# Relative attention on one core: distance terms turned into PSUM ahead of the products, two banks an image, constants loaded ahead of the norm

## The reference, cut to what matters

```python
x = layernorm(h)
q, k, v = x @ Wq + bq, x @ Wk + bk, x @ Wv + bv          # split in 8 heads
scores[i, j] = (q[i] . k[j] + q[i] . rel_k[clip(j - i)]) * scale
w = softmax(scores, axis=j)
y[i] = sum_j w[i, j] * (v[j] + rel_v[clip(j - i)])
h = h + y @ Wo + bo
```

## Time and profile before

| | us |
|---|---|
| Median of 3 runs | 2627.47 (2611.75 to 2633.1) |
| The profiled execution | 2611.67 |
| Its span, first to last instruction | 2609.9 |
| Granted clock of TensorE, mean over the span | 0.922 |
| Norm ahead of the stage, from the first table load | 1529.4 to 1557.0 |
| Relative attention: constants | 1557.9 to 1569.9 |
| Projections and far scores | 1569.9 to 1624.9 |
| Loop over the images | 1625.1 to 1791.6 |
| Values and outputs | from 1791.7 |

### The profile page before, as it was taken

How to read it: one execution, slowest core, us unless ns; L and a number is a source line. 1 busy time by engine, 2 the same in 40 slices (tenths; PEclk the granted TensorE clock), 3 DMA queues, 4 the chain that set the end, 5 groups by cost and what they waited for, 6 DMA issues and landing times. The chain is left out here.

```text
span 2609.9 us, 55965 instructions
## 1 busy us (share of the span) xinstructions
PE 2198.0 (84%) x22566; PEld 1555.1 (60%) x22566; DVE 1868.2 (72%) x2584; ACT 1619.1 (62%) x2458; POOL 570.5 (22%) x263
## 2 busy tenths in 40 slices
PE   5348999999999999999954958778569999999998
PEld 2135444454444444454323746664459999999998
DVE  0543888888888888888655445673668788888886
ACT  0025888888888888888751314332157777777776
POOL 0023444444444444444210001331000000000000
PEclk9658999999999999999865979999769999999999
DMA  4017777777777777777611000000122222212220
GB/s 172 0 45 199 210 204 213 220 208 218 216 205 206 211 215 217 209 219 216 166 41 41 1 8 3 1 1 21 66 72 77 74 69 69 69 69 74 71 69 34
DMA packets 110228, 306.64 MB, mean 117 GB/s; under 512 B 20334, under 2 KB 56936, under 8 KB 109209
## 3 DMA queue, kind: packets, MB, share of 16 engines
q1 hardware_dynamic: 109977, 303.11, 39.7%
HBM read 170.09 MB, written 80.65 MB: 96 GB/s over the span
## 5 line engine op out<-in xcount | busy, mean ns | idle before, releaser
L579 ACT ACTIVATE la_hid<-ps,la_b 128x904 f32<-128x904 f32 (+1 forms) x480 | 450.8, 988 | 72.6 <-PE ps L434 71.7
L1515 PE MATMUL ps<-ls_xm,ls_w_in_parts 128*128 128x226 f16 x3072 | 467.7, 261 | 13.2 <-DVE ls_xm L1596 9.0
L1523 PE MATMUL ps<-ls_state_parts,ls_w_rec_parts 128*128 128x226 f16 x2976 | 448.0, 259 | 0.0
L1542 ACT ACTIVATE ls_gates<-ps,ls_bias 128x226 f32<-128x226 f32 x768 | 301.6, 446 | 127.0 <-PE ps L1523 126.9
L434 PE MATMUL ps<-la_pairs,la_w 32*64 32x452 f32 x3584 | 311.0, 573 | 45.3 <-ACT la_hid L579 42.4
L1515 PEld LDWEIGHTS ps<-ls_xm,ls_w_in_parts 128*128 128x128 f16 x3072 | 294.5, 97 | 23.1 <-issue 9.3
L1523 PEld LDWEIGHTS ps<-ls_state_parts,ls_w_rec_parts 128*128 128x128 f16 x2976 | 285.2, 96 | 6.3
L447 PE MATMUL ps<-la_hid,la_w 128*32 128x452 f32 x1856 | 248.3, 560 | 1.0 <-ACT la_opened L585 1.0
L408 POOL TENSOR_TENSOR la_P<-la_S,la_top 113x904 f32<-113x904 f32 x64 | 153.3, 2395 | 263.9 <-DVE la_top L682 263.9
L434 PEld LDWEIGHTS ps<-la_pairs,la_w 32*64 32x64 f32 x3584 | 74.3, 131 | 186.4 <-issue 113.0
L396 POOL TENSOR_TENSOR la_P<-la_P,la_inv 113x904 f32<-113x904 f32 x64 | 132.1, 2085 | 189.7 <-DVE la_inv L661 189.7
(11 more groups left out here) (294 smaller groups left out, 4247.8 us busy)
## 6 DMA issues: line engine op xcount, KB each, us to landing
la_pairs<-la_maps SPq DMA_DIRECT2D x224, 452.0 KB, 6.1
la_gate<-la_opened SPq DMA_DIRECT2D x448, 113.0 KB, 3.4
ls_w_all<-ls_weights SPq DMA_DIRECT2D x32, 904.0 KB, 4.1
la_maps<-la_ST SPq DMA_DIRECT2D x32, 791.0 KB
la_maps<-la_S SPq DMA_DIRECT2D x32, 791.0 KB
ls_m_all<-ls_masks SPq DMA_DIRECT2D x32, 456.0 KB, 3.6
la_maps<-la_Cr SPq DMA_DIRECT2D x32, 395.5 KB
la_maps<-la_Cl SPq DMA_DIRECT2D x32, 395.5 KB
```

Source lines behind the costliest of these rows:

```text
L579: act.activation(hid[:, u % 4, 0:n], ps[:, bank:bank + n, 0:HALF], ACT.Gelu_apprx_tanh, bias=b1[:])\
L1515: mm = pe.matmul(out_j, w_in_parts[:, w, e, j, :], xm[:, t % 2, e, :, x, 0:N], start=((w, x) == PASSES[0]), stop=(t == 0 and (w, x) == PAS ...
L1523: mm = pe.matmul(out_j, w_rec_parts[:, w, e, j, :], state_parts[:, x, e], start=False, stop=((w, x) == PASSES[-1]))
L1542: return act.activation(dst, ps[:, n % 3 * 2 + j // 2, j % 2 * 256:j % 2 * 256 + C], ACT.Tanh if j == 3 else ACT.Sigmoid, bias=bias[:, e, ...
```

## The change

- The constants' tiles are made first, and a block of their own, with SyncE alone, loads them; then `norm_and_turn` runs, called from within `relative_attention`; then the rest. The other engines wait for `consts_in` where they did.
- GpSimd waits for `bias_set`, VectorE's signal after `q_bias`, before it adds `b_out` to `h`.
- The products of an image take two banks, four heads each, and there are three such sets (banks 0 to 5). Image b uses set b mod 3.
- `distances(b)` is new: eight transposes (`is_transpose`) of the distance terms into the image's two banks. It waits until image b - 3 is subtracted. `scores(b, part)` adds the products of q and k to them, in two halves of four heads; each half uses two of the four strips of rows, one strip a bank. The second waits for the first (`half_made`).
- `turn(b)` has one pair of banks, 6 and 7, in place of two, so it waits until image b - 1 is copied. The heads lie in another order in `z`, which `turn` undoes.
- TensorE's order: `distances(b)`, `scores(b, 0)`, `turn(b - 2)`, `scores(b, 1)`. The orders of VectorE and ScalarE stay.

```diff
     with Phase(nc, "ra") as ph:
...
+        consts_in = ph.sem("consts_in")
+        with ph.block() as block:
+            @block.sync
+            def _(sp):
+                for tile, name in loads:
+                    sp.dma_start(tile[:], dram[name]).then_inc(consts_in, 16)
+                for tile, name in rows:
+                    sp.dma_start(tile[:], dram[name].partition_broadcast(N)).then_inc(consts_in, 16)
+
+        norm_and_turn(nc, "ra_norm", h, hT, ps, ident, eps)
+
...
-                for tile, name in loads:
-                    sp.dma_start(tile[:], dram[name]).then_inc(s["consts_in"], 16)
-                for tile, name in rows:
-                    sp.dma_start(tile[:], dram[name].partition_broadcast(N)).then_inc(s["consts_in"], 16)
                 sp.wait_ge(s["scores_made"], B)
...
-                pool.wait_ge(s["consts_in"], ALL_IN)
+                pool.wait_ge(consts_in, ALL_IN)
+                pool.wait_ge(s["bias_set"], 1)
                 pool.tensor_tensor(h[:], h[:], b_out[:].unsqueeze(1).broadcast_to([N, B, D]), ALU.add).then_inc(s["bias_added"], 1)
...
-                def scores(b):
-                    if b >= 1:
-                        pe.wait_ge(s["shifted"], b)
+                def distances(b):
+
+                    if b >= SETS:
+                        pe.wait_ge(s["shifted"], b - SETS + 1)
+                    for bank in range(2):
+                        for part in range(2):
+                            for t in range(2):
+                                pe.matmul(ps[0:N, 2 * (b % SETS) + bank, slot(part, t)], weights[:, 4 * part + 2 * bank + t, b, :],
+                                          ident[0:N, 0:N], is_transpose=True, start=(part == 0 and t == 0), stop=False,
+                                          skip_group_check=True)
+
+                def scores(b, part):
+
+                    if part:
+                        pe.wait_ge(s["half_made"], b + 1)
                     for t in range(2):
-                        for j in range(4):
+                        for bank in range(2):
+                            j = 2 * part + bank
                             rows4 = slice(32 * j, 32 * j + 32)
-                            pe.matmul(ps[0:N, j, t * N:(t + 1) * N], q[rows4, t, b, :], kT[rows4, b, :],
-                                      start=(t == 0), stop=False, skip_group_check=True)
-                    for t in range(2):
-                        for j in range(4):
-                            mm = pe.matmul(ps[0:N, j, t * N:(t + 1) * N], weights[:, 2 * j + t, b, :], ident[0:N, 0:N],
+                            mm = pe.matmul(ps[0:N, 2 * (b % SETS) + bank, slot(part, t)], q[rows4, t, b, :], kT[rows4, b, :],
                                            start=False, stop=True, skip_group_check=True)
-                    mm.then_inc(s["scores_made"], 1)
+                    mm.then_inc(s["scores_made"] if part else s["half_made"], 1)
 
                 def turn(b):
                     pe.wait_ge(s["normed"], b + 1)
-                    if b >= 2:
-                        pe.wait_ge(s["weights_ready"], b - 1)
+                    if b:
+                        pe.wait_ge(s["weights_ready"], b)
                     for hd in range(H):
-                        tr = pe.transpose(ps[0:N, 4 + 2 * (b % 2) + hd // HB, hd % HB * N:(hd % HB + 1) * N],
-                                          z[:, b % 4, hd * N:(hd + 1) * N], ident[0:N, 0:N])
+                        part, bank, t = hd // 4, hd // 2 % 2, hd % 2
+                        place_of = 4 * bank + 2 * part + t
+                        tr = pe.transpose(ps[0:N, 6 + hd // HB, hd % HB * N:(hd % HB + 1) * N],
+                                          z[:, b % 4, place_of * N:(place_of + 1) * N], ident[0:N, 0:N])
                     tr.then_inc(s["turned"], 1)
...
                 for b in range(B + 2):
                     if b < B:
-                        scores(b)
+                        distances(b)
+                        scores(b, 0)
                     if b >= 2:
                         turn(b - 2)
+                    if b < B:
+                        scores(b, 1)
...
                 def largest(b):
                     dve.wait_ge(s["scores_made"], b + 1)
-                    x = ps[0:N, 0:4, 0:2 * N].rearrange("p j (t n) -> p j t n", t=2)
-                    signal(dve, dve.tensor_reduce(top[:, b % 2].rearrange("p (j t) -> p j t", t=2), x, AX_X, ALU.max), s["top_step"], b + 1)
+                    x = ps[0:N, 2 * (b % SETS):2 * (b % SETS) + 2, 0:HB * N].rearrange("p k (s n) -> p k s n", s=HB)
+                    top_b = top[:, b % 2].rearrange("p (k s) -> p k s", k=2)
+                    signal(dve, dve.tensor_reduce(top_b, x, AX_X, ALU.max), s["top_step"], b + 1)
...
-        norm_and_turn(nc, "ra_norm", h, hT, ps, ident, eps)
-        relative_attention(nc, h, hT, ps, ident, dram)
+        relative_attention(nc, h, hT, ps, ident, eps, dram)
```

More of the change, by code:

```diff
@@ L1050, in _, with relative_attention @@
                     add(q)
-def relative_attention(nc, h, hT, ps, ident, dram):
+def relative_attention(nc, h, hT, ps, ident, eps, dram):
     J = 2 * N - 1
@@ L1065, in relative_attention @@
     Q4 = 4
+    SETS = 3
     with Phase(nc, "ra") as ph:
         sb = ph.sb
+        w_q, w_k, w_v, w_out = (sb(n, [D, D]) for n in ("w_q", "w_k", "w_v", "w_out"))
+        b_q, b_k, b_v, b_out = sb("b_q", [D, 1]), sb("b_k", [D, 1]), sb("b_v", [N, D]), sb("b_out", [N, D])
+        rel_k, q_scale, q_bias = sb("rel_k", [D, J]), sb("q_scale", [D, 2]), sb("q_bias", [D, 2])
+        half_mask = sb("half_mask", [D, 2])
+        loads = [(w_q, "ra_w_q"), (w_k, "ra_w_k"), (w_v, "ra_w_v"), (w_out, "ra_w_out"), (b_q, "ra_b_q"), (b_k, "ra_b_k"),
+                 (rel_k, "ra_rel_k"), (q_scale, "ra_q_scale"), (half_mask, "ra_half_mask")]
+        rows = [(b_v, "ra_b_v"), (b_out, "ra_b_out")]
+        ALL_IN = 16 * (len(loads) + len(rows))
+        consts_in = ph.sem("consts_in")
[7 more added lines that the diff above has]
+        norm_and_turn(nc, "ra_norm", h, hT, ps, ident, eps)
         weights = sb("weights", [N, H, B, N])
@@ L1072, in relative_attention @@
         V = sb("V", [N, B, D])
[L1073 to L1076, removed]
         top, total, inv = sb("top", [N, 2, H]), sb("total", [N, 2, H]), sb("inv", [N, 2, H])
@@ L1087, in relative_attention @@
         yT = hT[:].rearrange("p b n -> p (b n)").rearrange("p (i w) -> p i w", i=8)
-        names = ("consts_in tables_in bias_set bias_added q_made kv_made q_ready kv_ready far_made far_act far_dve scores_made top_step "
+        names = ("tables_in bias_set bias_added q_made kv_made q_ready kv_ready far_made far_act far_dve half_made scores_made top_step "
                  "shifted raised sum_step inv_ready normed turned weights_ready y2_made y2_act y2_dve pick_made pick_act "
@@ L1092, in relative_attention, with slot @@
         s = {n: ph.sem(n) for n in names}
[L1093 to L1096, removed]
         def queries(u):
             return range(CHUNK * u, min(CHUNK * u + CHUNK, N))
-        def by_bank(x):
-            return x.rearrange("p (k c) -> p k c", k=2)
+        def slot(part, t):
+            return slice((2 * part + t) * N, (2 * part + t + 1) * N)
         def by_head(x):
@@ L1219, in outputs @@
                     mm.then_inc(s["out_made"], 1)
-                pe.wait_ge(s["consts_in"], ALL_IN)
+                pe.wait_ge(consts_in, ALL_IN)
                 for c in range(B // Q4):
@@ L1269, in _ @@
             def _(act):
-                act.wait_ge(s["consts_in"], ALL_IN)
+                act.wait_ge(consts_in, ALL_IN)
                 act.wait_ge(s["bias_set"], 1)
@@ L1287, in _ @@
                         act.wait_ge(s["turned"], b - 1)
-                        bank = 4 + 2 * (b % 2)
                         act.activation(weights[:, :, b - 2, :].rearrange("k (c h) n -> k c h n", c=2),
-                                       ps[0:N, bank:bank + 2, 0:HB * N].rearrange("p c (h n) -> p c h n", h=HB),
+                                       ps[0:N, 6:8, 0:HB * N].rearrange("p c (h n) -> p c h n", h=HB),
                                        ACT.Copy).then_inc(s["weights_ready"], 1)
@@ L1309, in largest @@
                     dve.wait_ge(s["scores_made"], b + 1)
-                    x = ps[0:N, 0:4, 0:2 * N].rearrange("p j (t n) -> p j t n", t=2)
-                    signal(dve, dve.tensor_reduce(top[:, b % 2].rearrange("p (j t) -> p j t", t=2), x, AX_X, ALU.max), s["top_step"], b + 1)
+                    x = ps[0:N, 2 * (b % SETS):2 * (b % SETS) + 2, 0:HB * N].rearrange("p k (s n) -> p k s n", s=HB)
+                    top_b = top[:, b % 2].rearrange("p (k s) -> p k s", k=2)
+                    signal(dve, dve.tensor_reduce(top_b, x, AX_X, ALU.max), s["top_step"], b + 1)
                     if b >= 4:
                         dve.wait_ge(s["turned"], b - 3)
[L1314 to L1317, removed]
```

(4 more changed lines are left out.)

## The result

The changed kernel takes 2709.84 us (median of 4, 2708.69 to 2711.02), the kernel before 2625.44 (median of 4): a ratio of 1.033 between the runs, interval 1.029 to 1.037 (the two medians alone give 1.032). The profiled execution took 2709.89 us, 98.2 more than that of before.

A forecast was written before the change was run, and what follows sets the result against it. The prediction took the per-image loop to be bound by a chain across engines, none full. It summed 2611.67 + 84.6 - 6.2 - 2.4 = 2687.7 us, lifted to 2692 for spread, range 2648 to 2714.

The forecast's parts named there:

- head and tail: Loop's start and end: the head loses some 0.4 us, the tail gains it back, so 0.
- (b): TensorE's order in the loop: turn's wait for GpSimd delays the next maximum, making a step 6.81 us at full clock.
- One sign: Expected in the new loop's profile: turn waiting about 4 us for GpSimd each time.
- (c): Loop's clock: transposes don't hold it, so the loop runs at 1.2 GHz with a step of 7.89 us.
- rival 1: Loop's clock stays at 2.4 GHz or mostly: 2655 us, or 2671 for a half-and-half mixture; chance 0.18.
- (d): Loop, first to last maximum: 2.2 us first step plus 30 x 7.89 gives 238.9 against 154.26, +84.6.
- The range's inner bounds: Main case's total, 2688 to 2704, widened to 2675 to 2712 by bounds on the products' 1.0 us half.
- (e): Constants loaded ahead of the norm: net 6.2 us faster, bounds 0.4 slower to 12 faster.
- (f): Projections: with q_bias ahead of GpSimd's addition, the third projection's wait goes, 2.4 us faster; bound 0.
- The spread: Whole kernel: the spread of runs would lift the changed kernel's median, so 2687.7 became 2692.
- Rival 2: In the loop VectorE sets the step at 3.47 us: 48.0 us faster, total 2555; chance 0.04.
- rival 3: Constants block's closing barrier waits for the landing: 0.4 us slower instead of 6.2 faster, 2694; chance 0.08.

The follow-up runs named there:

- Run 1: Changed kernel with turn(b-2) moved behind the second half of the products of b: 2626.9 us, ratio 1.003 to the kernel before.
- run 5: Changed kernel with GpSimd multiplying only four of the eight heads, part of the computation left out: 2693.6 us in one execution.
- run 7: Old-loop kernel of run 6 with distances turned in transpose mode, in the old banks and order: 2614.97 us, 10.2 more than with ordinary distances.
- the first kernel of run 9: Changed kernel without the far-score pause, next image's distances between the product halves, turn(b-2) last, by ordinary products: 2648.82 us, ratio 1.011.
- Run 4: Kernel before with only the constants and biases parts of the change, old loop kept: 2620.39 us, ratio 1.001.
- run 6: Far scores no longer wait for the last k and V: changed kernel 2698.56 us, ratio 1.028; old loop with constants and biases 2604.81, 0.993.

## Why the prediction was right, and where its sizes were off

The direction and the mechanism held, and the time lies in the range: 2709.8 us in 2648 to 2714, forecast 2692. That it lies inside is in part luck. On the profiled execution the sum was 2687.7 and the time 2709.9, 22.2 more: 12.5 in the loop's steps, 2.9 at its head and tail, 14.4 in the far scores, less 0.9 at constants and biases and less 6.7 in stages whose code is unchanged. Without these last 6.7, which nothing in the change explains, the time would have been above the range. By the prediction's own steps:

- *(b), the order.* Right. Run 1 takes it away and the loss goes, at the same clock 2.7 us of each step, and run 5 shows GpSimd's time in the step one for one. One sign was off: turn waits 2.6 us for GpSimd, not about 4. The 4 fits the step at full clock; at the low one TensorE spends longer on distances and first half, and less of GpSimd's time is left to wait for.
- *(c), the clock.* Right for this loop: 0.50 throughout, so rival 1, that it stays high, did not come. That turned distances can cost the clock though TensorE is busier is shown by the two loops of run 7. The Trainium skill, TensorE: Matmul & The Clock Gate, section PE-mode transpose, says that transpose mode doesn't count as busy in the same way; run 7 agrees with it (0.50 at 88% busy, 0.92 at 74%). As the reason that the prediction made of it, that only 0.8 us in a step hold the clock, it is too simple: run 1 has the same 0.8 us and was granted 0.72, and the first kernel of run 9 has ordinary turns besides and was granted 0.55.
- *(d), the loop's sum*, +97.1 measured for +84.6. Two terms were small. Turn to the next instruction is 1.79 us (1655.88 to 1657.67), not 1.55; products to the maximum 1.15 (1657.67 to 1658.82), not 1.04. That makes a step 8.25 us on average in place of 7.89, 10.7 us in 30 steps. And the first step took 4.00 us, not 2.2, as TensorE at 1.2 GHz is itself the slower one there (+1.8). I had read the low-clock durations from short slow stretches; the row shown is granted 0.57 and not 0.50, so probably part of it ran at full clock. The range's inner bounds were added up a little off: -10 and +9 to 2688 and 2704 give 2678 and 2713, not 2675 and 2712. Head and tail, set to 0, were +1.6 and +1.3.
- *(e), constants:* -6.3 for -6.2. *(f), biases:* -3.2 for -2.4. The wait is gone; 0.5 of the other 0.8 is the second projection of q, which took 1.45 us before, across the rise of the clock, and 0.92 after. q_bias took 8.90 us beside GpSimd's addition and 0.23 ahead of it, and the additions from PSUM took 0.69 beside it. The Trainium skill, SBUF — State Buffer, section Who interferes with whom, says that a tensor_scalar within SBUF can enter a mode in which it and GpSimd block each other, and that outside such modes a VectorE instruction with at most one SBUF input doesn't contend with GpSimd; these rows agree.
- *A step that was missing:* the far scores. I carried them over unchanged, without a reason; they cost +14.4, because the clock fell in them. Run 4 shows that this comes with (e) and (f), run 6 that it goes when the pause ahead of them goes.
- *The spread.* I lifted the forecast by 4 us because runs of the kernel before spread, over 21 us in its first four and over 26 to 33 in the longer series. The changed kernel's spread over 2.3, so the lift had no ground in it. Why is not shown: the turned loop of run 7 is at the low level throughout as well, and its runs spread over 13.5.
- *Rival 2 (VectorE paces the loop)* and *rival 3 (loads exposed)* did not come; the timelines above exclude both.

What stays open: why the pause ahead of the far scores comes with a fall of the clock in six profiles and not in the one of the kernel before, and why the loops of runs 1 and 7, with the same instructions for an image, were granted 0.72 and 0.50.

## What to carry to other kernels

Before buffers are added to put more in flight, write down for each engine what stands in its queue ahead of the instruction that the next stage waits for; a wait placed there puts the whole round trip into the step, however many buffers there are. Turning an ordinary product with the identity into transpose mode halved that work here (16 instructions to 8) and cost the clock of everything else in the loop in run 7; compare granted clocks, not instruction counts. A gain ahead of a stage counts only once the stage itself has been looked at again: a shift can change the clock at which it runs.

## What was unexpected of the hardware

The far scores, ordinary products on 32 rows and 64 columns, kept TensorE busy for 38 of 38 us in the changed kernel (1586 to 1624) and were granted 0.50 all that time; the same work was granted 1.00 for 26 of 26 us in run 6. In the changed kernel, too, they started at 1.00, and the clock fell 2 us after their start, with TensorE busy:

```profile
1583.00:1584.00 1.00, 1.00 (x41) 1.00 (x41) 0.00 (x0) 0.00 (x0) 0.00 (x0) 1.00 0.00 0
...
1585.00:1586.00 1.00, 1.00 (x31) 1.00 (x28) 1.00 (x1) 1.00 (x1) 0.00 (x0) 0.50 0.00 0
```

From there it stayed down to the end of the stage: 41.9 us, or 26.9 in run 6. Taking out a pause of 1.47 us ahead of the stage went together with the high level in all six profiles, but with the pause in place the kernel before was at 1.00 as well. So TensorE can be busy without a gap for 38 us and stay at the low level, and a pause of this length can be followed by a fall or not.
